# A graph network on one core: two long loops announce their branch late, and the source table of the edge stage goes from three bf16 parts to two float32r parts

## The reference, cut to what matters

```
edge_index = jnp.stack([src, dst])
h = jnp.maximum(_layernorm(x, axis=-1), 0.0)
x = x + _L0_gnn_ref(h, edge_index, W1, b1, W2, b2)          # hypergraph layer
h = jnp.maximum(_layernorm(x, axis=-1), 0.0)
x = x + _L1_gnn_ref(h, src, dst, edge_weight1, ...)          # edge layer

def _L1_gnn_ref(h, row, col, dist, ...):
    edge_in = jnp.concatenate([h[row], h[col], dist], axis=1)
    e = jax.nn.silu(edge_in @ eW1 + eb1)
    e = jax.nn.silu(e @ eW2 + eb2)
    agg = jax.ops.segment_sum(e, row, num_segments=h.shape[0])
    node_in = jnp.concatenate([h, agg], axis=1)
    return jax.nn.silu(node_in @ nW1 + nb1) @ nW2 + nb2
```

## Time and profile before

| what | value |
|---|---|
| time, median of 3 runs | 10372.06 us (10370.75 to 10374.2) |
| the profiled execution: its time, its span | 10401.59 us, 10399.8 us |
| mean granted TensorE clock over the span | 0.969 |
| TensorE busy, counting stage (1200 to 3000 us) | 1686.3 of 1800 us |
| VectorE busy there | 1684.2 of 1800 us |
| TensorE busy, edge stage (8600 to 10200 us) | 1561.6 of 1600 us |
| VectorE, ScalarE busy there | 1204.8, 803.8 of 1600 us |

### The profile page before, as it was taken

How to read it: one execution, slowest core, us unless ns; L and a number is a source line. 1 busy time by engine, 2 the same in 40 slices (tenths; PEclk the granted TensorE clock), 3 DMA queues, 4 the chain that set the end, 5 groups by cost and what they waited for, 6 DMA issues and landing times. The chain is left out here.

```text
span 10399.8 us, 323623 instructions
## 1 busy us (share of the span) xinstructions
PE 9642.0 (93%) x115049; PEld 8724.8 (84%) x115882; DVE 7564.4 (73%) x24984; ACT 4824.6 (46%) x9346; POOL 2440.9 (23%) x3828
## 2 busy tenths in 40 slices
PE   2999999999999998999899999959999999999997
PEld 2888888888888887999899999948888888888885
DVE  7999999999999996444455444357777777777773
ACT  1877877877877775000000000035555555555552
POOL 3555555455445542000000000001111111111110
PEclk9999999999999999999899999859999999999998
DMA  2323323322322325666577666453333333333332
GB/s 59 88 86 87 88 84 87 88 84 86 87 86 86 87 86 134 190 190 167 136 192 192 185 192 192 123 122 90 87 88 89 90 90 90 90 89 88 90 87 68
DMA packets 850047, 1149.67 MB, mean 111 GB/s; under 512 B 204300, under 2 KB 585462, under 8 KB 848004
## 3 DMA queue, kind: packets, MB, share of 16 engines
q1 hardware_dynamic: 818806, 1106.24, 38.2%
q0 software_dynamic: 28224, 26.62, 1.0%
q10 hardware_dynamic: 1840, 0.53, 0.0%
HBM read 774.19 MB, written 358.49 MB: 109 GB/s over the span
## 5 line engine op out<-in xcount | busy, mean ns | idle before, releaser
L794 ACT ACTIVATE RB<-PS 128x1024 fp8e4<-128x1024 f32 x2401 | 2438.5, 1024 | 557.0 <-PE PS L674 516.4
L555 POOL TENSOR_SCALAR OH<-iot,kd 128x102 bf16<-128x102 bf16 x3440 | 2029.5, 609 | 1787.4 <-DVE ddc L849 1751.6
L1886 POOL DMA_INDIRECT Qx<-tab_q,tidx x294 | 397.8, 1353 | 5665.1 <-DVE skt L1920 2894.2
L1170 PE MATMUL hp<-ACC,RG 128*128 128x193 bf16 (+1 forms) x19208 | 1634.9, 246 | 7.1 <-DMA RG<-adjT 7.1
L1170 PEld LDWEIGHTS hp<-ACC,RG 128*128 128x128 fp8e4 x19208 | 1620.5, 97 | 15.1 <-issue 8.0
L928 DVE TENSOR_SCALAR OU<-iot,SBk 128x256 bf16<-128x256 bf16 x4802 | 1397.0, 291 | 0.0
L672 PE MATMUL PS<-OU 128*128 128x256 bf16 x4802 | 1196.4, 275 | 171.6 <-DVE OU L928 128.0
L927 DVE TENSOR_SCALAR OU<-iot,SBk 128x128 bf16<-128x128 bf16 x4802 | 1250.6, 261 | 7.3 <-PE PS L674 7.1
L690 PE MATMUL HP<-T3a,RB 128*128 128x193 bf16 x9604 | 1201.4, 249 | 0.4 <-ACT RB L794 0.4
L674 PE MATMUL PS<-OU 128*128 128x128 bf16 x9604 | 1200.3, 220 | 0.0
L1962 DVE TENSOR_TENSOR Zb<-p,eb2s 128x512 f32<-128x512 f32 x882 | 610.0, 692 | 791.8 <-PE p L1859 763.0
(11 more groups left out here) (320 smaller groups left out, 15525.9 us busy)
## 6 DMA issues: line engine op xcount, KB each, us to landing
RG<-adjT SPq DMA_DIRECT2D x1372, 224.0 KB, 3.5
adj<-RB SPq DMA_DIRECT2D x343, 448.0 KB, 2.6
adjT<-RB SPq DMA_DIRECT2D x686, 224.0 KB, 3.4
RG<-adj SPq DMA_DIRECT2D x686, 224.0 KB, 3.5
sdb<-bk SPq DMA_DIRECT2D x196, 768.0 KB
sdb<-bk SPq DMA_DIRECT2D x98, 384.0 KB
sdb<-bk SPq DMA_DIRECT2D x98, 261.0 KB
WR<-wk SPq DMA_DIRECT2D x882, 9.0 KB
```

What stands on the lines that cost most here:

```text
L555: ins = e.tensor_scalar(OH[:, g * GT + k, :], iot1[:, 0:KEYS], kd[:, g * GT + k:g * GT + k + 1], None, ALU.is_equal)
L794: e.activation(RB[n % NSLOT][:, :, k, :], PS[u % 2][:, :].rearrange("p (a w) -> p a w", a=2), ACT.Copy, accum_out=gs[:, u:u + 1], saturate ...
L1170: ins = e.matmul(ps[b][:, h * W:(h + 1) * W], lhsT=RG[:, n, k_ * 256 + h * P:k_ * 256 + (h + 1) * P], rhs=tin3[:, n * 2 * PIECE + k_, 0:W] ...
```

## The change

In TensorE's counting loop and TensorE's edge loop, `hinted` is replaced by `announced`: the same loop, whose branch hint is issued where the body calls `mark()`. In the counting loop that is ahead of slice 12 of 14 in the pass's second turn; in the edge loop ahead of group 16 of 18. All other loops keep `hinted`.

In the edge stage the source table P is held in two float32r parts in place of three bf16 parts: a value rounded to float32r, and the rest. `tab_p`, `Pst`, `Pb` and the one-hot tile `OsT` change their types, the third part's matmul is dropped, and so are one copy on ScalarE and one subtraction on VectorE a group in the table stage. A bf16 one-hot of the source is still needed for `Qb` in a block's ninth group; it is now written by VectorE into 144 columns of `OdT`.

```
+        @contextmanager
+        def announced(e, a, b):
+            on = bass.OrderedEngineSet([e.engine])
...
+            with nc.body(f"{name}_body", valid_engines=on):
+                yield nc.snap(at, min_val=a, max_val=b - 1), lambda: marks.append(e.mark_branch_hint_location())
+                nc.regs_alu(at, at, 1, op=ALU.add)
+                e.br_lt(at, b, on_true=f"{name}_body", on_false=f"{name}_end").branch_hint(marks[0])
...
-                        with hinted(e, 1, NCH // 2) as j:
+                        with announced(e, 1, NCH // 2) as (j, mark):
                             turn(j * 2 + 1, True, True, True, True)
-                            turn(j * 2 + 2, True, True, True, True)
+                            turn(j * 2 + 2, True, True, True, True, mark)
...
-            Pst = [sbt(tx, f"Pst{n}", [P, GB, 3, HID], bf16) for n in range(3)]
-            rP = [sbt(tx, f"rP{n}", [P, GB, HID], fp32) for n in range(2)]
+            Pst = [sbt(tx, f"Pst{n}", [P, GB, 2, HID], f32r) for n in range(3)]
...
-                            e.activation(Pst[q % 3][:, :, 1, :], rP[q % 2][:, :, :], ACT.Copy)
...
-                            e.tensor_tensor(rP[g % 2][:, :, :], sums(pP2, g), Pst[g % 3][:, :, 0, :], ALU.subtract)
+                            e.tensor_tensor(Pst[g % 3][:, :, 1, :], sums(pP2, g), Pst[g % 3][:, :, 0, :], ALU.subtract)
...
-                            e.tensor_tensor(Pst[q % 3][:, :, 2, :], rP[q % 2][:, :, :], Pst[q % 3][:, :, 1, :], ALU.subtract)
...
-            Pb = [sbt(cx, f"Pb{n}", [P, 3, HID], bf16) for n in range(2)]
+            Pb = [sbt(cx, f"Pb{n}", [P, 2, HID], f32r) for n in range(2)]
...
-            OsT = [sbt(cx, f"OsT{n}", [P, 512], bf16) for n in range(2)]
+            OsT = [sbt(cx, f"OsT{n}", [P, 512], f32r) for n in range(2)]
...
-                                    ins = e.matmul(o[:, a:b], lhsT=Qb[q][:, c, :], rhs=S_[:, a:b], start=False, stop=True, skip_group_check=True)
+                                    ins = e.matmul(o[:, a:b], lhsT=Qb[q][:, c, :], rhs=D_[:, 0, a:b], start=False, stop=True, skip_group_check=True)
...
-                            for c in range(3):
+                            for c in range(2):
                                 ins = e.matmul(o[:, :], lhsT=Pb[q][:, c, :], rhs=S_[:, :], start=False, stop=True, skip_group_check=True)
...
-                        skewed(e, [[(1, stage_t)], [(2, stage_2)], [(4, stage_a)]], NGF, FTURNS)
+                        skewed(e, [[(1, stage_t)], [(2, stage_2)], [(4, stage_a)]], NGF, FTURNS, NGF - 3)
...
+                            if wd < 512:
+                                a, b = span(AT_D, AT_X, g)
+                                ins = e.tensor_scalar(OdT[g % 2][:, 0, a:b], v[:, 0, at + a:at + b], pio[:, 0:1], None, ALU.is_equal)
```

More of the change, by code:

```diff
@@ L2 @@
 from concourse import mybir
-from contextlib import ExitStack
+from contextlib import ExitStack, contextmanager
 import math
@@ L83, in hinted @@
             return nc.Fori(a, b, engines=bass.OrderedEngineSet([e.engine]), hint_back_edge=True)
+        @contextmanager
+        def announced(e, a, b):
+            on = bass.OrderedEngineSet([e.engine])
+            name = f"announced{nc.next_id()}"
+            at = nc.alloc_registers(f"{name}_i", engines=on)
+            marks = []
+            nc.regs_mov(at, a)
+            nc.br(f"{name}_body", engines=on)
+            with nc.body(f"{name}_body", valid_engines=on):
+                yield nc.snap(at, min_val=a, max_val=b - 1), lambda: marks.append(e.mark_branch_hint_location())
+                nc.regs_alu(at, at, 1, op=ALU.add)
+                e.br_lt(at, b, on_true=f"{name}_body", on_false=f"{name}_end").branch_hint(marks[0])
+            nc.switch_bb(f"{name}_end")
         def past(e, s, v):
@@ L104, in gnn_kernel @@
         gt_agg = dram("gt_agg", (ROWS, HID), fp32)
-        tab_p = dram("tab_p", (ROWS, 3 * HID), bf16)
+        tab_p = dram("tab_p", (ROWS, 2 * HID), fp32)
         pay = dram("pay", (3, EP), fp32)
@@ L711, in step, with turn @@
                                 sums(i - 1, u - 3)
-                        def turn(i, rank, unit, tail, before):
+                        def turn(i, rank, unit, tail, before, mark=None):
                             for g in range(NGR):
+                                if mark and g == NGR - 3:
+                                    mark()
                                 k, us = units(i, g, unit, tail)
@@ L1612, in _ @@
                         e.dma_start(tab_p.rearrange("(b p) f -> p b f", p=P)[:, g * GB:(g + 1) * GB, :],
-                                    Pst[g % 3][:, :, :, :].rearrange("p j c h -> p j (c h)")).then_inc(u_d[g % 3], 16)
+                                    Pst[g % 3][:, :, :, :].rearrange("p j c h -> p j (c h)").bitcast(fp32)).then_inc(u_d[g % 3], 16)
                         e.dma_start(tab_q3.rearrange("(b p) f -> p b f", p=P)[:, g * GB:(g + 1) * GB, :],
@@ L1681, in gnn_kernel, with skewed, turn @@
             sem(f"l_{n}") for n in ("oh", "ob", "w", "t", "tc", "p", "y", "2", "zb", "z", "a", "add"))
-        def skewed(e, slots, ngl, turns):
+        def skewed(e, slots, ngl, turns, soon=None):
             depth = max(n for slot in slots for n, _ in slot)
-            def turn(i, first, last):
+            def turn(i, first, last, mark=None):
                 for g in range(depth if last else ngl):
+                    if mark and g == soon:
+                        mark()
                     for slot in slots:
@@ L1694, in skewed @@
             turn(0, True, False)
-            with hinted(e, 1, turns) as i:
-                turn(i, False, False)
+            if soon is None:
+                with hinted(e, 1, turns) as i:
+                    turn(i, False, False)
+            else:
+                with announced(e, 1, turns) as (i, mark):
+                    turn(i, False, False, mark)
             turn(turns, False, True)
@@ L1788, in turn @@
                                 done(e, l_p, i, (q - 1) * GB9 - 1)
-                                e.dma_start(Pb[q][:, :, :], tab_p[DS(i * (2 * P) + q * P, P), :].rearrange("p (c h) -> p c h", c=3)).then_inc(l_pl[q], 16)
+                                e.dma_start(Pb[q][:, :, :].bitcast(fp32), tab_p[DS(i * (2 * P) + q * P, P), :].rearrange("p (c h) -> p c h", c=2)).then_inc(l_pl[q], 16)
                                 e.dma_start(Qb[q][:, :, :], tab_q3[DS(i * (2 * P) + q * P, P), :].rearrange("p (c h) -> p c h", c=3)).then_inc(l_pl[q], 16)
@@ L1996, in gnn_kernel @@
             xf = sbt(cx, "xf", [P, 1], fp32)
-            xP = sbt(cx, "xP", [P, 3 * HID], bf16)
+            xP = sbt(cx, "xP", [P, 2 * HID], fp32)
             xQ = sbt(cx, "xQ", [P, HID], fp32)
@@ L2120, in _ @@
                                 e.tensor_tensor(xB[:, :], x2[:, 0:HID], nW["eb2s"][:, :], ALU.add).then_inc(x_e, 1)
-                                e.wait_ge(l_add, s0 + 6)
+                                e.wait_ge(l_add, s0 + 5)
                                 e.wait_ge(x_m, j * M8 + (m + 1))
```

4 lines of the change are left out of this document (2 added, 2 removed).

## The result

| what | before | after |
|---|---|---|
| time, median of 4 runs each | 10373.13 us (10370.75 to 10376.16) | 10263.99 us (10262.22 to 10264.63) |
| ratio, 95% interval | | 0.9894 (0.9877 to 0.9911) |
| profiled execution: its time, its span | 10401.59, 10399.8 us | 10264.35, 10262.4 us |
| counting loop on TensorE: branch, pass, packets a pass | 3649 ns, 158.1 us, 14 | 3408 ns, 157.5 us, 14 |
| edge loop on TensorE: branch, pass, packets a pass | 1956 ns, 65.78 us, 9 | 216 ns, 63.49 us, 0 |

The kernel is faster by 109 us, where 241 were forecast. The time lies inside the range, but it is that of the second rival (10252 us), not of the first. The two profiled spans differ by 137 us and not by 109, since the profiled execution of before took 28 us more than its median; so I read passes and branches, not ends.

What follows compares the result with a forecast made beforehand. TensorE alone bounds the edge stage; in the counting stage TensorE and VectorE hold each other up. From 10401.6 us, -110 - 20 - 110 = -240 gives 10161.6; the median lies 29.5 lower, so 10132 us, range 10070 to 10270.

Steps and rivals of the forecast that it cites:

- the second rival: Both loops: the hint's place changes nothing, only float32r pays, with 0 to 20 us from the edge loop; 10252 us, chance 0.28.
- the first: Whole kernel: both late hints and the float32r part all work; 10132 us, range 10062 to 10187, chance 0.55.
- what a stall costs: Counting loop on TensorE: a back edge costs 5.1 us, slow clock included, and 22 cost 112 us.
- the late hint in the counting loop, -110 us: Counting loop on TensorE: the branch falls from 3649 to 208 ns, the queue hides it, 110 us saved.
- the full effect: Counting loop: the late hint brings the branch down to the short loop's 208 ns; given 0.6.
- the two things said against the effect: Edge branch is 1.7 us shorter under the same early hint; the skill's sequential-prefetch rule makes the hint's place worth 0.
- the edge loop's back edge, -20 us: Edge loop on TensorE: the late hint removes the visible back-edge idle time, 20 us, bounds 0 and 23.
- the third rival: Edge loop: late hint misses or shorter body misplaces the branch, which stalls 3.6 us; kernel slower, 10480 us, chance 0.08.
- Its second condition: Edge loop, third rival: a stall this long needs both the hint and the shorter body to fail.
- the float32r part, -110 us: Edge stage on TensorE: two float32r matmuls for three bf16 save 125 ns a group, 110 us over 882.
- The row with "118 ns, 104 us": Edge stage: the first float32r weight load comes about 95 ns late behind a short matmul, the second hides.
- the costs of nothing: VectorE's one-hot grows 140 to 300 ns under its wait for p, cost 0; table stage 0 us, within 3.

Runs made afterwards that it cites:

- e1: The kernel after with both hints put back at the top of their loops, float32r part kept; ratio 0.9887 to the kernel before.
- e3: The kernel after with TensorE's counting loop rolled to one turn a pass, 1671 instructions for 3342; ratio 0.9809 to the kernel before.
- e5: The kernel after with the two-turn counting loop begun at instruction 150 of its packet, without a hint there; ratio 0.9892 to the kernel before.
- e4: The kernel after with the two-turn counting loop begun at instruction 150 of its packet, hint at the top; ratio 0.9785 to the kernel before.
- e2: The kernel before with the late hints in both loops and nothing else, three bf16 parts kept; ratio 1.0001 to the kernel before.
- e10: The kernel after with the edge loop's hint at the top and its head at instruction 20 of a packet; ratio 1.0001 to the kernel before.
- e7: The kernel after with a one-turn counting loop and the edge loop begun at place 0 without a hint; ratio 0.9905 to the kernel before.
- e9: The kernel after with a one-turn counting loop and the edge loop begun at place 0, hint at the top; ratio 0.9781 to the kernel before.
- e11: The kernel after with WR's 512-column bf16 matmul moved to just ahead of Pb's, part of the result left out; ratio 0.9813 to the kernel before.
- e13: The kernel after with each edge group's Pb matmuls first and WR's last, everything summed; ratio 0.9834 to the kernel before.

## Why the prediction was right or wrong

**Right: what bounds, and nearly what a stall costs.** The back edge costs 5.1 us in the counting loop, slow clock included, I had said. It measured 4.4 us from e1 to e3 (157.8 - 153.4) and 3.5 from e5 to e4 (157.4 - 153.9), where the start of the body is the same too. Some luck is in the 5.1: its turn of 76.6 us lies above both turns that it names (76.1 and 76.5, which would give 5.7), and e3's turn then took 76.69. What TensorE drops in the edge stage is gained: its 2.29 us a pass came whole into the time.

**Wrong: the late hint in the counting loop, -110 us.** The step that failed: "A hint at the top is issued while the head is there; a hint three slices or groups from the end is issued when it is gone", on which "I put 0.6 on the full effect". The counting branch stayed at 3.4 to 3.6 us with 14 packets in the kernel after and e1, and e1 and e2 show that the place is worth nothing in either loop. The starts of the instruction packets show why: the fetch that ends the stall begins at the same moment with either hint, a median 1.02 us behind the start of the counting branch before and 1.01 after, and 0.59 us ahead of the edge branch before and 0.54 in e2. So the late hint starts nothing earlier. The second rival had this case, with 10252 us; it came to 10264, partly by luck, since its 110 and 10 us were 88 and 22. Of the two things said against the effect, one was the sentence to weigh more: a hint at the top already made the edge branch shorter than the counting one, so "where it stands may not be what counts". The rule of the Trainium skill that the prediction set beside it (Runtime: NRT & Kernel Launch, "Instruction fetch mechanics"), that code is prefetched in sequence and a taken branch outside the window waits, was right on this place, with 3649 and 3408 ns in the two kernels. That there is a hint is another matter: e4 against e5 shows that it can be worth 3.2 us a branch.

**Right in size, wrong in cause: the edge loop's back edge, -20 us.** It gave 0.48 us a pass, 22 us. But what healed it is that 36 instructions went, so that the body and its start fit in the eight packets that stay, and that the loop has a hint at all. e3 (another start) and e10 (20 places on) lose it, e7 (no hint) too. The same section of the Trainium skill gives TensorE's instruction window as 128 KiB, 2048 instructions; e9 and e10, with 2042 instructions from place 0 and 20, agree. I had noted the shorter body only as something that might put the branch in a worse place, in the third rival. That rival was no fancy: e10 has its stall, a branch of 3.3 us, by a start 20 instructions later. It costs 2.45 us a pass, 115 us, and not 5.1: the clock stood at 1.2 GHz for 41 of the 2600 us from 7,200 to 9,800 only. With the float32r part won, e10 is as fast as the kernel before (ratio 1.0001), not slower. Its second condition, "a stall this long needs both the hint and the shorter body to fail", was too strong; the place alone does it.

**Mis-sized: the float32r part, -110 us.** It measured 100 ns a group, 88 us, where I took 125. The term that was off is the extra of the second matmul and the exposed load together. The first matmul takes 316 ns, 101 more than bf16's 215, near the 95 ns that I had read off the weight loads; the second takes 229, 14 more. The row with "118 ns, 104 us" had the mechanism, which e11 and e13 show, and lacked those 14 ns. I had chosen a value between it and a cheaper case. My estimate from the 107 ns that the Trainium skill's page TensorE: Matmul & The Clock Gate ("LDWEIGHTS") gives for a load left some 70 ns exposed; the row's 95 was nearer.

**Right: the costs of nothing.** VectorE's one-hot went up by 133 ns, just under my 140 to 300, and of its wait for `p` 0.65 us a group were left. The table stage moved by 2 us at most.

**What stays open.** What starts a hinted fetch. When it starts can be read off the trace, if the last packet of the instruction queue that starts before the end of a branch is the one that it waits for. The DMA view's row of that queue, for the window of three branches in which this packet starts: e4's counting branch at 1603.8 us (1599 to 1600), before's edge branch at 8036.8 (8035.8 to 8036.8), before's counting branch at 1315.9 (1315.9 to 1317.9):

```profile
q8 instruction: 1, 0.02, 5.8%
q8 instruction: 1, 0.02, 8.0%
q8 instruction: 1, 0.02, 3.3%
```

| loop | packet starts, from the branch's start (median) | branch |
|---|---|---|
| no hint: e5 counting, e7 edge | 1.01, 1.04 us behind | 3578, 3760 ns |
| before, counting | 1.02 us behind | 3649 ns |
| e10, edge | 0.76 us behind | 3307 ns |
| e3, edge | 0.35 us ahead | 2007 ns |
| before, edge | 0.59 us ahead | 1956 ns |
| e4, edge | 0.98 us ahead | 1405 ns |
| e4, counting | 4.49 us ahead | 349 ns |

Where the branch stalls it ends 2.4 to 2.6 us after that start, so what the loop's place changes is when the fetch begins. One reading of why: the hinted fetch begins when TensorE's sequencer, which reads its instructions, enters the packet that holds the branch. By the counts the branch lies 14 instructions into its packet in e10 and some 160 in e4's counting loop, and the order fits. The amount does not quite: 160 instructions at 46 ns each (153.9 us / 3342) are 7 us, and the fetch starts 4.5 us ahead. Where the other loops' branches lie in their packets is not on record. So this is argued and not shown: no run varied that place in steps. Nor was a hint tried that stands in the branch's own packet.

## What to carry to other kernels

Count the instructions of a hot loop on each engine before and after an edit, and look at the instruction packets of one pass and at the closing branch: a loop just over what stays can lose more by 20 instructions than an arithmetic change wins, and a long body cut in half (e3) no longer stalls. Then look at the loops behind it too, since they move. When a change moves two things, the one that pays may be the code's length. Here a matmul whose weight load is long was cheaper behind a matmul of 256 or 512 columns than behind one of at most 84; reordering so won more (1.16 us a pass in e13) than the back edge of that loop did.

## What the runs showed of the hardware that I had not expected

- A loop on TensorE of 2042 instructions runs with no instruction packet fetched when it begins at place 0 and its branch is hinted (e9: 223 ns). Without the hint the same loop fetches 9 packets a pass and stalls 3760 ns (e7).
- The hint's own place in the body changes nothing (e1: 223 ns at the top in the edge loop; after: 216 late; 3613 and 3408 ns in the counting loop).
- With a body that is fetched anew each pass, 14 or 15 packets, the branch costs 349 ns or 3578 ns by the hint alone (e4, e5).
- A branch of 1.4 us in a loop that fetches 9 packets a pass costs it 0.09 us (e4, edge). With branches of 2.0 us the clock stayed at 2.4 GHz over the whole edge stage (before, e3), with 3.3 us it stood at 1.2 GHz for 41 of 2600 us (e10), with 3.8 us for 61 (e7).
- A float32r matmul of 512 columns starts the next one 229 ns later, bf16's 215; behind a short matmul the first costs 101 ns more than bf16, behind 256 columns two take 0.47 us together (e13).
